# Layer 0's relation transform as f32 matmuls on two row halves, in a graph kernel on one core

## The reference

```python
h = maximum(layernorm(x), 0)
x = x + aggregate(h * src_norm)[dst] * dst_norm          # layer 0: plain graph sum
h = maximum(layernorm(x), 0)
for l in range(2):                                       # layers 1 and 2: relational
    seg = dst * 65 + edge_type
    mean = segment_sum(h[src], seg) / maximum(count(seg), 1)
    conv = relu(einsum('nrd,rdk->nk', mean, W[l]) + h @ root[l] + bias[l])
    h = conv + relu(h @ res_W[l] + res_b[l])
x = x + h
```

## Time and profile before

| what | value |
|---|---|
| runs | 10352.16, 10351.77, 10351.72 us (median 10351.77) |
| profiled execution, span | 10352.2 us, equal to the slowest run |
| PE, DVE, ACT, POOL busy | 4552.1, 5431.7, 2301.0, 7615.4 us |
| mean granted clock of PE | 0.654 of full speed |
| layer 0's turns | from about 512 to 2417 us |

### The profile page before, as it was taken

One profiled execution on the slowest core, in us unless ns is written; L12 is line 12 of the kernel. 1 busy time (PEld: TensorE's weight loads), 2 busy tenths in 40 slices (PEclk: granted clock), 3 DMA queues, 4 the chain that ended last, 5 costly groups with the idle time before them and its releaser, 6 DMA issues.

```text
span 10352.2 us, 181683 instructions
## 1 busy us (share of the span) xinstructions
PE 4552.1 (44%) x39273; PEld 3343.3 (32%) x39273; DVE 5431.7 (52%) x20234; ACT 2301.0 (22%) x5818; POOL 7615.4 (74%) x8147
## 2 busy tenths in 40 slices
PE   4489888985444444444444444222222222222222
PEld 3366666663222222222222222222222222222222
DVE  9877676766777766767767675222222222222222
ACT  7856666562111111111111111000000000000000
POOL 6577777775777777777777776777777777777777
PEclk8889999997666666666666666555555555555555
DMA  3234444445444444444444444111111111111112
GB/s 89 61 129 147 140 144 142 142 145 167 138 148 148 144 145 145 148 148 139 147 148 143 146 145 138 30 30 30 30 30 30 30 30 30 30 30 30 30 30 41
DMA packets 535833, 1017.81 MB, mean 98 GB/s; under 512 B 243588, under 2 KB 289684, under 8 KB 534340
## 3 DMA queue, kind: packets, MB, share of 16 engines
q1 hardware_dynamic: 255956, 745.88, 19.9%
q0 software_dynamic: 253216, 261.57, 13.1%
q10 hardware_dynamic: 25872, 2.47, 0.3%
HBM read 559.43 MB, written 454.23 MB: 98 GB/s over the span
## 4 chain that ended last, share of the span: by engine, by line
POOL 61%; issue 23%; PE 8%; DVE 4%; ACT 1%; DMA 1%; ACTq 1%; SPq 1%; POOLq 0%; DVEq 0%
POOL rows L890 33%; POOL w_parts L890 28%; PE y_ps L1272 3%; PE block_ps L1359 2%; DVE ystage L1600 2%; PE sums_ps L1324 1%; PE y_ps L1351 1%; ACT scr L1028 1%; ACTq L323 1%; PE signs_ps L1351 0%; SPq L323 0%; DMA y_table<-ystage 0%; DVE onehot L1635 0%; DMA rows<-h_table,idx_st 0%; DVE w_raw L1781 0%
## 5 line engine op out<-in xcount | busy, mean ns | idle before, releaser
L890 POOL DMA_INDIRECT rows<-y_table,idx_st x3136 | 2961.1, 944 | 1038.8 <-issue 1038.8
L890 POOL DMA_INDIRECT w_parts<-y_table,idx_st x3163 | 2987.2, 944 | 964.8 <-issue 964.5
L1706 DVE TENSOR_SCALAR rr<-rr 128x64 f32<-128x64 f32 x198 | 42.2, 213 | 4070.2 <-PE block_ps L1301 4070.2
L1467 PE MATMUL sums_ps<-onehot,rows 128*64 128x64 f32 x6468 | 759.2, 315 | 2624.1 <-DMA rows<-y_table,idx_st 2549.2
L1467 PE MATMUL sums_ps<-w_parts 128*64 128x64 f32 x6424 | 751.8, 315 | 2556.1 <-DMA w_parts<-y_table,idx_st 2519.8
L890 POOL DMA_INDIRECT rows<-h_table,idx_st x1452 | 1398.5, 963 | 552.4 <-issue 451.2
L1467 PEld LDWEIGHTS sums_ps<-onehot,rows 128*64 128x64 f32 x6468 | 706.6, 223 | 2704.2 <-DMA rows<-y_table,idx_st 1603.1
L1467 PEld LDWEIGHTS sums_ps<-w_parts 128*64 128x64 f32 x6424 | 705.3, 224 | 2629.7 <-issue 2213.1
L994 ACT ACTIVATE idx_st<-edges 128x11 int32 (+1 forms) x720 | 141.6, 211 | 5571.5 <-PE sums_ps L1467 3103.6
L1018 ACT ACTIVATE ystage<-y_ps 128x512 f32<-128x512 f32 (+1 forms) x1782 | 1009.4, 568 | 988.9 <-PE y_ps L1272 833.4
L1645 DVE TENSOR_SCALAR_CACHE_REDUCE w_raw<-edges,step_key 128x384 bf16<-128x384 f32 x1568 | 850.5, 605 | 15.6 <-DVE step_key L1625 15.6
(11 more groups left out here) (231 smaller groups left out, 6433.8 us busy)
## 6 DMA issues: line engine op xcount, KB each, us to landing
y_table<-ystage SPq DMA_DIRECT2D x396, 768.0 KB, 3.7
edges<-key_row SPq DMA_DIRECT2D x198, 832.0 KB, 5.6
rows<-y_table SPq DMA_DIRECT2D x9408, 0.2 KB
y_table<-ystage SPq DMA_DIRECT2D x198, 608.0 KB, 3.3
w_parts<-y_table ACTq DMA_DIRECT2D x6272, 0.2 KB
w_raw<-key_row SPq DMA_DIRECT2D x99, 832.0 KB
w_parts<-y_table,idx_st POOLq DMA_INDIRECT x3163
rows<-y_table,idx_st POOLq DMA_INDIRECT x3136, 2.5
```

The costliest lines, as they stand in the source:

```text
L890: pool.indirect_dma_start(out=rows_of(l, u)[:, j, k, 0:D], out_offset=None, in_=table, in_offset=bass.IndirectOffsetOnAxis(ap=idx_of(l, u, ...
L1467: ins = nc.tensor.matmul(sums_ps[u][0:width, c:c + W], rows_of(l, u)[:, j, k, 0:width], onehot_of(l, u)[:, j, k, :], start=False, stop=False)
```

## The change

- **Y of layer 0.** `whole_chunk` replaces `transform_chunk`: one f32 matmul over 64 rows, h and weights in f32, not split. The weights stay in `w_raw` as loaded (twice, in rows 0 to 63 and 64 to 127), h is there twice too (`h_twice`, `hT_whole`), and even and odd chunks use one row half each. The last chunk of a block always uses the lower one.
- **Banks and order.** Y uses four banks, `signs_ps` and `deg_ps` as well. Four chunks are issued in a row, then the part of the apply that belongs to them (4/18 or 4/9 of it). Tile group 2 comes after 12 of 18 parts.
- **h.** DVE writes the normalized block twice in f32, one instruction in place of five; PE turns it with one f32 transpose in place of two bf16 ones; ACT's copy takes the maximum with 0 (Relu) and has 128 columns of f32.
- **Weights.** `split_w` for layer 0 is gone. Layer 1's weights are loaded into `w_scr` (the memory of `w_parts`) and split from there. The far one-hots of the counting, and `same` and the third key buffer of layer 1, move from `w_raw` to `w_scr`; the second buffer of tile rows in layers 1 and 2 is `w_raw`.
- **Steps.** BODY is (1, 0, 1, 1, 1, 0, 1, 1), six bodies. That gives Q = 42 gathered blocks and NH = 56 counted ones: a first turn, 48 in bodies, and seven more: 1, 0, 0, 1, 1, 1, 1. 42 turns gather, 14 are alone.

```diff
-    BODY = (1, 0, 1, 1, 1, 1, 0, 1, 1, 1)
+    BODY = (1, 0, 1, 1, 1, 0, 1, 1)
...
-        odd_home = (w_raw[:, :], w_scr, w_scr)
+        odd_home = w_raw[:, :]
...
+        turned_h = [sums_ps[u][:, 2 * P:3 * P] for u in range(2)]
+        h_twice = flat(h_parts).bitcast(f32)
+        hT_whole = [hT[:, v, :, :].rearrange("p a n -> p (a n)").bitcast(f32) for v in range(2)]
...
+        y_banks = (y_ps[0], y_ps[1], signs_ps, deg_ps)
...
+            def copy_whole_hT(s, v, turned):
+                act.wait_ge(hT_done[0], s + 1 + 1)
+                nc.scalar.activation(hT_whole[v], turned, ACT.Relu).then_inc(hT_ready[0], 1)
...
+            def turn_whole_h(s, turned):
+
+                pe.wait_ge(h_ready[0], s + 1 + 1)
+                nc.tensor.transpose(turned, h_twice, ident[:, :]).then_inc(hT_done[0], 1)
+
+            def whole_chunk(s, c, v, at):
+
+                if at + c >= 4:
+                    pe.wait_ge(y_read[0], s * YC + c - 2)
+                lastc = c == YC - 1
+                half = 0 if lastc else (at + c) % 2 * D
+                n, bank = y_cols(c), y_banks[(at + c) % 4]
+                ins = nc.tensor.matmul(bank[:, 0:n], hT_whole[v][half:half + D, :],
+                                       w_raw[half:half + D, c * BANK:c * BANK + n], start=True, stop=not lastc)
+                if lastc:
+                    o = R * D - c * BANK
+                    ins = nc.tensor.matmul(bank[:, o:o + 2 * D], ones[:, :], brow[:, D:3 * D],
+                                           start=False, stop=True)
+                ins.then_inc(y_done[0], 1)
...
-                    for n, v in ys:
-                        pe.wait_ge(hT_ready[0], n + 1)
-                        for c in range(YC):
-                            transform_chunk(0, n, c, v)
-                            if at == 0:
+                    for first in range(0, parts, 4):
+                        for c in range(first, min(first + 4, parts)):
+                            n, v = ys[c // YC]
+                            if c % YC == 0:
+                                pe.wait_ge(hT_ready[0], n + 1)
+                            if c == 2:
                                 pe.wait_ge(hist_by_act, m * ACT_EVICTS + ACT_EVICTS)
                                 pe.wait_ge(hist_by_dve, m * DVE_EVICTS + DVE_EVICTS)
...
+                            whole_chunk(n, c % YC, v, c // YC * YC)
+                        if first == 0:
+                            if more:
+                                pe.wait_ge(slots_read, m + 2)
+                            else:
+                                pe.wait_ge(applied_read, m + 1)
+                        apply_part(m, NBK * first // parts, NBK * min(first + 4, parts) // parts)
+                        if tiles_of and first <= parts // 2 < first + 4:
+                            add_tiles(*tiles_of)
...
-                step(V.tensor_scalar(h[:, :], x_of(at), mv[:, 0:1], col[:, 2:3], ALU.subtract, ALU.mult))
-                split_h(0, n)
+                dve.wait_ge(hT_done[0], n + 1)
+                two = x_sb[:, at, :].unsqueeze(1) if isinstance(at, int) else x_sb[:, bass.ds(at, 1), :]
+                V.tensor_scalar(h_twice.rearrange("p (a d) -> p a d", a=2), two.to_broadcast([P, 2, D]),
+                                mv[:, 0:1], col[:, 2:3], ALU.subtract, ALU.mult).then_inc(h_ready[0], 1)
...
-                split_w(0)
...
-                split_w(1, 2)
+                split_w(1, w_scr[:, 0:YW], 2)
```

More of the change, by code:

```diff
@@ L220, in gnn_kernel @@
         sq = w_scr[:, 0:2 * QB * D].rearrange("p (a b d) -> p a b d", a=2, d=D)
-        same = w_raw[:, KR * P:].bitcast(bf16)[:, 0:KS * 3 * P].rearrange("p (k n) -> p k n", k=KS)
+        same = w_scr[:, KR * P:].bitcast(bf16)[:, 0:KS * 3 * P].rearrange("p (k n) -> p k n", k=KS)
         if ETP >= 2 * KR * P:
@@ L283, in rows_of @@
                 return rows
[L284 removed]
+            return odd_home[:, 0:RC].rearrange("p (j k d) -> p j k d", j=J, k=K)
         def onehot_of(l, u):
@@ L614, in load_weights_row_by_row @@
                     for half in (0, D):
-                        sp.dma_start(w_raw[half:half + D, :], w1_table).then_inc(w_loaded[1], 16)
+                        sp.dma_start(w_scr[half:half + D, 0:YW], w1_table).then_inc(w_loaded[1], 16)
                 def last_turn(now):
@@ L1005, in copy_hT, with emit_whole_y @@
                   .then_inc(hT_ready[l], 1)
+            def copy_whole_hT(s, v, turned):
+                act.wait_ge(hT_done[0], s + 1 + 1)
+                nc.scalar.activation(hT_whole[v], turned, ACT.Relu).then_inc(hT_ready[0], 1)
+            def emit_whole_y(s, u, i, at):
+                for g in range(YG):
+                    n = YG * u + g
+                    act.wait_ge(y_saved[0][n % 2], (i * YG + n // 2 + 1) * 16)
+                    for c in range(g * SG, min(g * SG + SG, YC)):
+                        act.wait_ge(y_done[0], s * YC + c + 1)
+                        o = (c - g * SG) * BANK
+                        nc.scalar.activation(ystage[:, n % 2, o:o + y_cols(c)],
+                                             y_banks[(at + c) % 4][:, 0:y_cols(c)], ACT.Copy).then_inc(y_read[0], 1)
             def emit_y(l, s, u, i, parts=range(YG), copied=False):
@@ L1071, in act_turn @@
                         if f == 9 and now is not FIRST:
-                            copy_hT(0, now.n - 1, 1 - now.y, t_of[1 - now.u])
+                            copy_whole_hT(now.n - 1, 1 - now.y, turned_h[1 - now.u])
                         if f == 9 and now.gathers:
@@ L1405, in pe_turn @@
                             pe.wait_ge(hT_ready[0], n - 1)
-                            turn_h(0, n - 1, turned=t_of[1 - now.u])
+                            turn_whole_h(n - 1, turned_h[1 - now.u])
                         if k == 6 and gathers:
@@ L1409, in pe_turn @@
                                 pe.wait_ge(hT_ready[0], n)
-                            turn_h(0, n, turned=t_of[1 - now.u])
+                            turn_whole_h(n, turned_h[1 - now.u])
                         if gathers and k <= 6 and not first:
@@ L1421, in _ @@
                 pe.wait_ge(tr_read, 4 * TG)
+                pe.wait_ge(w_loaded[0], 16 * 6)
                 pe_turn(FIRST)
```

49 lines of the change are left out of this document (21 added, 28 removed).

## The result

The changed kernel takes 10279.2 us (median of 4 runs, 10277.7 to 10280.2), the kernel before 10351.7 (4 runs, 10349.8 to 10352.2). The ratio is 0.993, with a 95% interval of 0.9917 to 0.9943. That is 72.6 us faster; 91.8 were forecast. The time lies in the range on record and 19 us above its middle.

A forecast was written before the change was run, and what follows sets the result against it. POOL and PE were taken as almost level in layer 0, with POOL's gathers and waits summed. Layer 0's gathers ending 85.8 us earlier and 6 off the tail gave 10352.2 - 91.8 = 10260.4, told as 10260 us; range 10220 to 10312.

The forecast's parts named there:

- Y in pairs: Layer 0's Y on PE: f32 chunks on two row halves overlap in full, four chunks in 2.0 us where they took 2.6.
- A: Rival on PE's Y: passes don't pair at once, 0.43 us more per group of four chunks; 10297 us, chance 0.13.
- Rival C: PE's Y without overlap: chunks run one after another, PE alone sets the pace; slower, 10452 us, chance 0.07.
- Start: Layer 0's start: without the weight split on DVE, turn 1 starts 15.4 us earlier; POOL loses 13 in place of 25.3.
- Gathering turn: PE's turn with a gathered block: 33.9 us falls to 32.1, 1.1 from Y and 0.7 from the counting half.
- Rival B: Y no faster as a whole, evictions waiting for stores to free `ystage`; turns keep 33.9 and 27.1; 10306 us, chance 0.12.
- D: PE much faster: gathering plus alone turn fall by another 5.8 us, POOL's waits vanish; 10190 us, chance 0.05.
- E: Does nothing: lower granted PE clock and y stores colliding with gathers eat 4 us a turn; 10350 us, chance 0.05.
- W: POOL's wait for PE at an alone turn: 8.9 us on average before, 5.8 forecast at each of 11 more.
- The gather's pace: POOL in layer 0: 1.243 us per gather, 1386 gathers, 1722.8 us in all.
- The waits: POOL's waits for PE in layer 0: 11.9 us at the first, 63.8 at eleven more, 31.6 at the double alone turn.
- The 0.7 that I carried: POOL's wait at an alone turn: derived as 8.2 us where 8.9 was measured; the 0.7 was added to the forecast wait.

The follow-up runs named there:

- one_half: The changed kernel with every chunk of Y on the lower row half, so no two overlap: 10542.3 us, ratio 1.0181 against the kernel before.
- steps_only: The kernel before with only the new order of steps (42 gathered, 56 counted blocks), Y still in bf16: 10348.9 us, ratio 1.0001 against the kernel before.
- fill_alone: The changed kernel with extra PE matmuls of zeros in alone turns to hold the clock up: 10301.9 us, ratio 0.994 against the kernel before.
- two_to_one: The changed kernel with BODY (1, 0, 1, 1, 0, 1), 40 gathered and 58 counted blocks: 10273.0 us, ratio 0.9913 against the kernel before.

## Why the prediction was right, and where it was off

**Right, and shown.** Faster, by the mechanism named.

- *Y in pairs:* the two halves start together and passes 0.43 us apart, 1.92 us for four chunks; without overlap the change loses 1.8% (`one_half`). Rivals A and C fall.
- *Start:* turn 1 at 542.5 (543); the slow gathers lose 12.9 us in place of 25.3 (13); putting the split back costs 16.7.
- *Gathering turn:* 31.6 where 32.1 was said. From the first matmul of Y to the fold the shortest turns went from 21.76 to 20.81, a gain of 0.95 for the 1.1 of the forecast. The counting half gave 1.3 (a median of 12.2 to 10.9) where I took 0.7: PE's waits for the counts' eviction, in front of the first Y, went from 2.0 to 0.3.
- *Rival B* falls: fewer waits for stores, not more. *D* and *E* fall too: the two kinds of turn together came out 2.3 us shorter, not 5.8 more than my 3.1, and the alone turn's clock is 0.81 as before.
- *Rival C* was priced too low: without the overlap the kernel takes 10542, where I had 10452, since its alone turns are 33.6 and not 29.4 and I knew nothing of the rounds' starts.
- *W:* I said 5.8, and eleven waits measure 5.6 to 6.8, 6.0 on average.
- *Layers 1 and 2* unmoved (7909.4 for 7907.1). Over the kernels of this study that stretch is 7905 to 7923 us, so single spans compare only to some 5 to 10.

**Mis-sized.** The span is 16.3 us above my 10260.4, and the terms are these:

- *The gather's pace, +9.7.* I took the 98.5 us that the group puts down to PE as waits. They hold the 0.30 that POOL stands before every gather. The waits proper are 90.3, so (1931.0 - 90.3 - 25.3) / 1452 = 1.250 and not 1.243; two gathers that follow each other in the timeline above also start 1.25 apart. Times 1386.
- *The waits, +5.0.* 12.8 for 11.9, 66.3 for 63.8, 33.2 for 31.6. Behind it stands the step that failed: "turns of 33.9 - 1.8 = 32.1 and 27.1 - 1.3 = 25.8". I took the gain on PE's work off the alone turn without asking which engine ends it. It is DVE, with PE (part of it at the lower clock) only 0.5 us ahead, and the turn stayed 27.1. The kernel before had shown it: the fold that ends the alone turn of the earlier trace rows follows on DVE's work without a pause.

```profile
790.59 2.23 DVE L1781 TENSOR_TENSOR w_raw<-t_ps,rr 128x1024 bf16<-128x1024 bf16 x4
792.75 0.34 DVE L1755 TENSOR_REDUCE agg<-block_ps 128x64 f32<-128x192 f32 x1
```

That this cost so little is chance: the gathering turn came out 0.5 shorter, and the slower gathers left POOL 0.3 less to wait per four groups. The 0.7 that I carried without knowing its cause was mostly these 0.30s too (W before is 8.1 without them), and stood in for a part of what was missing.

- *Small ones:* a wait for ACT that I carried and that is gone (-2.1), the first gather 0.7 earlier, 0.5 of rest; the tail 50.4 for 48.8 (+1.6), layers 1 and 2 +2.3.

**Right for an incomplete reason.** I wrote that two engines are almost level, and then priced the steps on POOL alone, with W as the only thing that PE can do to it. `steps_only` shows what that leaves out: with the old Y the same steps move the time by nothing that can be measured, since PE's turns are longer (34.5 in the median) than the 33.9 that I read, one of the shortest. In the changed kernel the sum held because PE then had the room.

**Open.** What the 2.2 us are for which PE stands at the start of a round of the loop wasn't tried beyond making rounds longer. And the change to Y has parts that no run takes apart: the f32 matmuls, the four banks, and four chunks ahead of each part of the apply. `one_half` keeps the last two and is slower than the kernel before, so the overlap is needed. But how much of the turn's gain the f32 matmuls give, and how much the new order with its shorter waits for the counts, isn't shown.

## What to carry to other kernels

Before a gain on one engine is taken off a stage, look at the instruction that ends the stage: if the engine that issues it has no idle time before it, the stage belongs to that engine, however busy another is. When two engines are level, shifting work between them and making one faster are worth less apart than together (10 and 36 us of layer 0, together 78), so a shift should be tried again after each gain. Read the length of a stage as a median over all its turns: the first clean one here was 33.9 us, and the median 34.5.

## What the runs showed of the hardware that was not expected

- f32 matmuls on 64 rows each, on the two row halves, overlap also at 512 columns: two chunks in some 0.97 us, and 1.83 one after another.
- Holding TensorE's granted clock at 1.00 with matmuls of zeros cost time, some 12 us of layer 0 in `fill_alone`. The stage was not PE's, PE then stood 2.69 us for DVE, and the clock was 0.72 from 735.9 to 740 us, in a turn that was PE's: those turns grew from 31.6 to 32.5.
- Where one round of the loop follows another, PE stands 1.6 to 3.7 us in every kernel (2.21 in the row shown), and in `two_to_one` such a turn is 3.2 to 4.2 us longer. It costs time only where PE is on the path.
- A gather on POOL beside DVE's block of f32 multiplications took 14.19 us in place of 0.94, one instruction long, while the next was at 0.94 again.
